# An adaLN transformer block on one core: two quarters of the block mask are loaded and summed before the first pieces of the modulation matrix

## The reference, cut to what matters

```python
mod = (_silu(L0_c) @ L0_wmod).reshape(1, 6, 1, -1)            # c: 1 x 1024, wmod: 1024 x 6144
sa, ca, ga, sb, cb, gb = (mod[:, i] for i in range(6))
ga = (2 * (ga >= 0) - 1) * jnp.maximum(jnp.abs(ga), 0.25)      # gb likewise
bm = mask.reshape(32, 32, 32, 32).sum(axis=(1, 3)) > 0         # int32 mask, blocks of 32 x 32
w  = (weight.reshape(32, 32, 32, 32) * bm[:, None, :, None]).reshape(1024, 1024)
h = _layernorm(x) * (1 + ca) + sa                              # x: 2048 x 1024
x = x + ga * (h @ w.T + bias)
h = _layernorm(x) * (1 + cb) + sb
x = x + gb * ffn(h)      # gate, up (2752 x 1024 int32) and down weights with scales, silu(gate) * up
```

## Time and profile before

| | |
|---|---|
| device time, median of 3 runs | 1269.39 us |
| lowest and highest run | 1269.1 and 1271.07 us |
| span of the profiled execution, first to last instruction | 1267.0 us |
| mean granted TensorE clock over the span, share of full speed | 0.985 |
| PE busy | 1173.0 us (93% of the span) |
| DVE, ACT, POOL busy | 40%, 26%, 13% |
| DMA | 119.31 MB, mean 94 GB/s |

### The profile page before, as it was taken

One profiled execution on the slowest core, in us unless ns is written; L12 is line 12 of the kernel. 1 busy time (PEld: TensorE's weight loads), 2 busy tenths in 40 slices (PEclk: granted clock), 3 DMA queues, 4 the chain that ended last, 5 costly groups with the idle time before them and its releaser, 6 DMA issues.

```text
span 1267.0 us, 16256 instructions
## 1 busy us (share of the span) xinstructions
PE 1173.0 (93%) x4976; PEld 549.5 (43%) x4976; DVE 507.8 (40%) x645; ACT 330.3 (26%) x589; POOL 164.7 (13%) x170
## 2 busy tenths in 40 slices
PE   0476788999989999999999999999999999999998
PEld 0333443455444444444444444444444444444443
DVE  5769977866666444222222222122222222122222
ACT  2203257766643333200121210011121002111100
POOL 4415434544430000000000000000000000000000
PEclk9987899999999999999999999999999999999999
DMA  9998157887792333411000021100002110000010
GB/s 318 202 344 231 34 156 210 241 219 202 183 327 64 101 101 87 133 58 57 1 0 0 0 83 50 56 11 0 0 0 83 50 49 17 0 0 0 16 50 33
DMA packets 88549, 119.31 MB, mean 94 GB/s; under 512 B 17105, under 2 KB 59601, under 8 KB 88529
## 3 DMA queue, kind: packets, MB, share of 16 engines
q1 hardware_dynamic: 78112, 101.74, 28.5%
q0 software_dynamic: 4608, 16.78, 3.5%
q10 hardware_dynamic: 5808, 0.55, 0.4%
HBM read 93.87 MB, written 25.17 MB: 94 GB/s over the span
## 4 chain that ended last, share of the span: by engine, by line
PE 79%; DVE 10%; DMA 4%; issue 2%; SPq 2%; ACT 1%; DVEq 1%; POOL 1%; POOLq 0%; ACTq 0%
PE pA L865 43%; PE pB L883 23%; PE pA L785 10%; DVE wgu L992 2%; DMA wgu<-in_L_attn_weight 2%; PE pB L775 1%; DVE work L992 1%; DVE gbs L992 1%; DMA work<-in_L_wmod 1%; SPq L377 1%; DMA wgu<-in_L_wmod 1%; SPq L384 1%; PE pA L873 1%; DVE work L962 1%; DVE wgu L990 1%
## 5 line engine op out<-in xcount | busy, mean ns | idle before, releaser
L865 PE MATMUL pA<-work,wgu 128*128 128x512 f16 x2688 | 581.3, 379 | 4.8 <-DVE work L1137 2.9
L865 PEld LDWEIGHTS pA<-work,wgu 128*128 (+1 forms) x2688 | 262.8, 98 | 322.5 <-issue 6.3
L883 PE MATMUL pB<-work 128*128 128x512 f16 x1344 | 295.3, 379 | 1.2 <-DVE work L1137 1.2
L785 PE MATMUL pA<-work 128*128 128x512 f32 x512 | 232.5, 611 | 20.6 <-ACT work L624 11.1
L883 PEld LDWEIGHTS pB<-work 128*128 x1344 | 131.5, 98 | 159.9 <-issue 1.7
L1133 DVE SCALAR_TENSOR_TENSOR pA<-pA,small,work 128x512 f32<-128x512 f32 x84 | 63.7, 759 | 322.8 <-ACT work L700 322.8
L785 PEld LDWEIGHTS pA<-work 128*128 128x128 f32 x512 | 98.8, 197 | 139.1 <-issue 116.3
L700 ACT ACTIVATE work<-pA,small 128x512 f32<-128x512 f32 x84 | 57.6, 685 | 312.6 <-PE pA L865 312.5
L624 ACT ACTIVATE work<-pB,small 128x128 f32<-128x128 f32 x256 | 93.1, 481 | 141.7 <-PE pB L775 69.4
L1164 DVE SCALAR_TENSOR_TENSOR work<-pB,work 128x512 f32<-128x512 f32 x32 | 22.1, 692 | 225.1 <-ACT work L728 225.1
L1137 DVE SCALAR_TENSOR_TENSOR work<-work,pA 128x512 f32 (+1 forms) x84 | 57.7, 687 | 83.0 <-ACT work L702 83.0
(11 more groups left out here) (98 smaller groups left out, 458.6 us busy)
## 6 DMA issues: line engine op xcount, KB each, us to landing
wgu<-in_L_wmod SPq DMA_DIRECT2D x10, 2048.0 KB, 15.3
work<-in_L_ffn_gate_w SPq DMA_DIRECT2D x84, 128.0 KB, 5.2
work<-in_L_ffn_up_w SPq DMA_DIRECT2D x84, 128.0 KB, 5.2
work<-in_L_ffn_down_w SPq DMA_DIRECT2D x96, 112.0 KB, 2.4
work<-in_L_attn_data SPq DMA_DIRECT2D x16, 512.0 KB, 5.2
x_scratch<-work POOLq DMA_DIRECT2D x16, 512.0 KB, 5.2
h_scratch<-work POOLq DMA_DIRECT2D x16, 512.0 KB, 3.9
work<-h_scratch SPq DMA_DIRECT2D x16, 512.0 KB, 5.3
```

Of the source, the lines that this page charges most:

```text
L785: last = pe.matmul(pA[:, 2 * t.par + h, :], hT1[t.par][:, c, :], wT[:, c, h * H:(h + 1) * H], start=(c == 0), stop=(c == KT - 1))
L865: last = pe.matmul(pA[:, 2 * k + g, :], wgu_u[:, 2 * c + g, P * kc:P * (kc + 1)], hT[:, s, kc], start=(kc == 0 and s == 0), stop=(kc == KT ...
L883: pe.matmul(pB[:, 2 * k + s, :], h2[:, s, c, bass.ds(P * ts, P)], wd[:, c, k * H:(k + 1) * H], start=(c == 0), stop=(c == FT - 1 and s == 1))
```

## The change

SP issues the eight DMAs of mask quarters 0 and 1 right after the first tile of x, ahead of pieces 0 to 3 of `wmod`; they stood behind piece 3. DVE sums them after the layernorm of tile 0 and before `sum_half(0, 0)`; they stood after `sum_half(1, 0)`. PE adds up the blocks of both quarters before `columns(0)`, not after it. Nothing is added or removed.

```diff
@@ sync
             load_x(Tile(0, 0))
+            load_mask(0)
+            load_mask(1)
             load_piece(0)
             load_piece(1)
             load_x(Tile(0, 1))
...
             for pair in range(NQ // 2):
                 for q in (2 * pair, 2 * pair + 1):
-                    load_mask(q)
+                    if pair:
+                        load_mask(q)
@@ tensor
             transpose(0, Tile(0, 0))
-            columns(0, colp[:, 0:KT])
             mask_total_of(0)
             mask_total_of(1)
+            columns(0, colp[:, 0:KT])
             columns(1, colp[:, KT:2 * KT])
@@ vector
             norm1(Tile(0, 0))
+            mask_sums(0)
+            mask_sums(1)
             dve.wait_ge(silu_c_done, 1)
             sum_half(0, 0)
...
             for pair in range(NQ // 2):
                 even, odd = 2 * pair, 2 * pair + 1
-                mask_sums(even)
-                mask_sums(odd)
+                if pair:
+                    mask_sums(even)
+                    mask_sums(odd)
                 mask_of(even)
```

## The result

| | before | changed |
|---|---|---|
| device time, median of 17 runs | 1269.51 us | 1274.38 us |
| lowest and highest run | 1267.04 and 1273.49 us | 1270.77 and 1280.1 us |
| ratio, 95% interval | | 1.0035 [1.0024, 1.0046] |
| span of the profiled execution | 1267.0 us | 1272.7 us |

The change makes the kernel slower by 4.4 us (1269.5 x 0.0035), between 3.0 and 5.8. The forecast was 5.3 us.

A forecast was written before the change was run, and what follows sets the result against it. Bound: the head's chain to quarter 0's turn. Pieces 8.5 us late put POOL's product at 59.8; the 2.2 us meeting makes 62.0, the transpose's 2.26 makes 64.3 against 58.98: +5.3, 1274.7 us, range 1270.6 to 1277.4.

The forecast's parts named there:

- What bounds: Head of the kernel: the end moves with the moment quarter 0 is turned, 58.98 us before the change.
- The delay S: Pieces 0 to 3 and the second x tile land 8.5 us later behind the mask loads; ends 7.2 and 9.0.
- rival C: Pieces hardly later: if a DMA engine's lag goes, piece 3 comes 3.5 to 5.5 us later; 1269.4 to 1271; chance 0.15.
- POOL's way: Piece 3 at 42.7, ACT's scaling, POOL's sums from 47.8, then its product, ending at 59.8 alone, 62.0 with the meeting.
- Rival A: DVE and POOL do not meet in the head: quarter 0 turned at 62.1, +3.1 us, 1272.5 us; chance 0.18.
- The meeting: DVE's product of quarter 1 starts inside POOL's sums after the weight lands at 51.5; it holds POOL about 2.2 us.
- Work costed at nothing: DVE's row sums, PE's mask matmuls and DVE's mask bits (done by 47.6, after the second modulation sum at 47.1): no cost.
- both places are covered: DVE's two row sums, 2.28 us each, lie ahead of a wait in old and new place: nothing lost or won.
- The slack of 5.4 us: POOL's masked quarter 0 was ready at 51.30 and needed by the second transpose at 56.72: 5.4 us in hand.
- The signs named in advance: Changed profile: ACT on piece 3 at 42 to 43.5, DVE's product at 51 to 52, about 5 us idle before second transpose.
- A shift at 64 us: Quarter 0's turn, near 64.3 us, is 5.3 us later, and the same shift is found again at 210 us.
- PE and what follows: PE's first attention matmuls start 6 to 7 us later; its 1.81 us wait for the second pair takes up the excess.

The follow-up runs named there:

- the pure delay: Kernel before the change with one extra transpose of quarter 1 (2.3 us of DVE) ahead of the two; 1270.94 us, ratio 1.0027.
- experiment 3: Changed kernel, but DVE's product of quarter 1 reads the block totals from PSUM and compares them itself, one input in SBUF; 1269.85 us, ratio 1.0013.
- experiment 9: Changed kernel with one added wait: POOL starts its second modulation sum only when DVE has ended its own; 1273.37 us, ratio 1.0033.
- experiment 1: Kernel before with only the loads of mask quarters 0 and 1 moved first, DVE and PE order kept; 1278.97 us, ratio 1.0085.
- 2: Kernel before with only the load of mask quarter 0 moved first, DVE and PE as before; 1274.22 us, ratio 1.0042.
- 6: Changed kernel, DVE's product reading PSUM, early bits, POOL's quarter 0 product before its second sum, PE adding quarters 2 and 3 before attention; 1271.96 us, ratio 1.0027.
- experiment 7: Kernel of experiment 6, with POOL also waiting for the end of DVE's second modulation sum before its product; 1266.88 us, ratio 0.9993.

## Why the prediction was right

*What bounds.* Right. The turn of quarter 0 sets the end, one for one within the noise of the rest: the table shows it over ten kernels, and the pure delay agrees (3.4 us, 1.8 to 4.9, for 2.3).

*The delay S.* Predicted 8.5 us for all pieces. Piece 0 came 8.3 later. Piece 3, which is the one that counts, came at 40.0, 5.8 later than in the first profile of before, for 42.7 forecast. The error lies in the reference: its 34.2 held a late end of the load that other executions don't have. On the means of the executions (32.0 before, 39.4 changed) the delay is 7.4. Against the third execution of before (28.9), the two changed ones (40.0 and 38.8) are 10 to 11 later. My rival C had seen the lag, and taken it as something that the new order might remove. It comes and goes in the old order; in the eight executions with at least one quarter in front, piece 3 came 5.7 to 6.5 us behind piece 2, and 5.8 to 8.6 in the six others.

*POOL's way.* Piece 3, ACT, POOL's sums, the product: this is what the chain of the first changed profile goes through. POOL's product ended at 59.5 where 62.0 was forecast, mostly the 2.7 us by which S was smaller. But it was not the only way to the products, see the work costed at nothing. Rival A, no meeting, put the turn at 62.1 for POOL's sake; in experiment 3, without a meeting, it came at 60.44, and DVE's late bits set it.

*The meeting.* Priced at 2.2 us; POOL's product took 5.68, not 3.64: 2.0. In the second execution DVE lost the race and its product took 5.70, not 2.29: 3.4. Place wrong: I had it inside POOL's sums at 51.5 us, and it took place at the products at 53.6. It is there in experiment 9 as I had described it. The forecast had DVE's product wait for a weight that lands at 51.5; in fact it waited for the bits. Experiment 3 takes the meeting away and leaves 1.0013 of 1.0035.

*Work costed at nothing.* The second modulation sum of DVE was to end at 47.1. It ended at 53.3, shut out by POOL from 45.1. It was a near miss: undisturbed, the sum takes 7.3 us from 39.36 (as in experiment 9), so DVE needed 1.5 us more. This is the step of the prediction that failed: the bits, costed at nothing and forecast for 47.6, were ready at 53.5, where POOL's sums ended at 53.87 in the first execution and at 52.59 in the second. So two ways of almost the same length led to the products, and in the second execution the bits came last. The estimate from experiment 9 puts their price at 0.5 and 3.6 us in the two; with early bits and the meeting the mean turn would be 60.8, 2.3 us over the 58.4 of before. The other 2.1 us of the measured 4.4 then come from a shut-out that the forecast did not have. No run keeps the changed kernel's order on POOL and has the bits early without an added wait, so this stays an estimate. In experiments 1, 2 and 6 the same shut-out was on the path. The step "both places are covered" for the row sums was right for the change as a whole, and experiment 1 shows that with the new loads the old place would have cost some 6 us more (1.0085 against 1.0035).

*The slack of 5.4 us* was right for the first profile, and for the second of before (POOL's product ended at 50.36 and was needed at 55.92: 5.6). In the third, POOL waited 4.88 us for the bits, and DVE and POOL met at the products already; the turn came at the same time by another way. So the price of the change is right in sum partly by luck: S was smaller than forecast, the late bits made up for it, and the base has a meeting of its own in some executions.

*The signs named in advance.* Most of them missed. DVE's first modulation sum ended at 28.5, as said (28 to 29). ACT started on piece 3 at 40.02 and, in the second execution, at 38.80, where 42 to 43.5 was forecast and anything before 40 was to mean that the prediction is wrong. DVE's product started at 53.6 and not at 51 to 52; the wait ahead of the second transpose was 1.19 us and none, not about 5. A shift at 64 us was to be found again at 210: 2.9 us at the turn were 2.0 at 204 in the first pair of profiles. The total was near; the timetable under it was not.

*PE and what follows.* PE waited 2.4 us for the second pair in the changed kernel, so it gave no delay of its own. Where its first matmuls came still later (experiment 7, 65.6 us) it did.

## What to carry to other kernels

When loads are moved forward, what they push back is what counts: here 2 MB of mask, whose sums had 5.8 us to spare in the first profile before the weight came, went ahead of 8 MB on which three engines hang in a row. Follow each engine's path from the pushed transfers to the next common point, not the one that the chain shows alone, and look where VectorE and GpSimd then run side by side; reading one VectorE operand from PSUM took such a meeting away (2.8 us in the changed kernel; in the kernel before, nothing that the time shows). A near miss counts too: 1.5 us of DVE's work left when POOL began became 8.2. One profile is one execution: a slack read from it holds only if a second execution has it too.

## What the runs showed of the hardware

- A VectorE and a GpSimd instruction with two inputs in SBUF each shut each other out whole, and a lead of 0.08 us (POOL's) or 0.25 us (DVE's) decided who pays: DVE's L328 5.70 us and POOL's 3.64, or DVE's 2.44 and POOL's 5.68. With one of DVE's inputs in PSUM: 2.29 and 3.64. The Trainium skill says of such a pair that whichever starts first has the shared port for its whole instruction and the other waits (SBUF — State Buffer, section on two separate sides), and the rows agree.
- Many short DVE instructions beside long ones of POOL fared worst: 14 of them took 7.3 us when they ended ahead of POOL's second sum, and 13.9 to 17.2 where POOL caught the last few.
- The same loads in the same order landed up to 5.3 us apart from one execution of the kernel before to the next (piece 3 at 28.9 and 34.2), though the first of the load's 16 marks came at 27.7 to 28.0 in all three.
- TensorE's clock fell to its lower level at about 215 and 386 us in one execution of the changed kernel (mean granted clock 0.66 over 215 to 220, 0.83 over 380 to 390) and in neither place in another, with the same instructions ahead. A fall between 208 and 221 us was there in three of 14 executions, the three with the longest rest (1210.8 to 1211.7 against 1206.8 to 1209.3). What decides it stays open.
